# Cross-attention and mixture-of-experts layer: layer-norm statistics, bias split and weight pieces placed elsewhere, fewer index copies

## What is computed

```python
def reference(x, ctx, abundance, w_in, b_in, w_out, b_out, gate_w, expert_bias, w1, w2, w3):
    # x [2, 1024, 256], ctx [2, 64, 256], 16 heads of 16, 8 experts, hidden 704, top 2
    q = layernorm(x) @ w_q.T + b_q;  k = ctx @ w_k.T + b_k;  v = ctx @ w_v.T + b_v
    scores = einsum('bhqd,bhkd->bhqk', q, k) / 4 + log(abundance)[:, None, None, :]
    x = x + (softmax(scores) @ v) @ out_proj_weight.T + out_proj_bias
    xf = layernorm(x).reshape(2048, 256)
    s = softmax(xf @ gate_w.T);  sel = top_k(s + expert_bias, 2)
    # tokens sorted by expert; routed = xf[token] * s[token, expert]
    # out[token] += (silu(routed @ w1[e]) * (routed @ w3[e])) @ w2[e]
    return x + out
```

## Time and profile before

| what | us |
|---|---|
| median of 3 runs (lowest, highest) | 438.52 (437.52, 440.04) |
| the profiled execution | 439.58 |
| its span, from the first instruction to the last | 437.8 |
| PE, DVE, ACT, POOL busy | 354.1, 240.5, 197.6, 237.0 |

### The profile page before, as it was taken

How to read it: one execution, slowest core, us unless ns; L and a number is a source line. 1 busy time by engine, 2 the same in 40 slices (tenths; PEclk the granted TensorE clock), 3 DMA queues, 4 the chain that set the end, 5 groups by cost and what they waited for, 6 DMA issues and landing times.

```text
span 437.8 us, 9846 instructions
## 1 busy us (share of the span) xinstructions
PE 354.1 (81%) x2573; PEld 266.7 (61%) x2574; DVE 240.5 (55%) x615; ACT 197.6 (45%) x343; POOL 237.0 (54%) x295
## 2 busy tenths in 40 slices
PE   2676699999888862128899999999999999999830
PEld 1455578888876752115567776767677767776620
DVE  1655776576665247925555555555555555555400
ACT  3567477787877632004333334333344444333300
POOL 6319786675775755041345565655555555664340
PEclk9886898898999655558999999999999999999995
DMA  7923676767895721023777777777777777889546
GB/s 235 317 26 96 187 213 162 198 184 162 241 214 167 238 60 20 0 73 64 122 125 135 136 138 136 135 134 135 133 134 134 135 138 130 133 136 143 95 57 204
DMA packets 121523, 61.53 MB, mean 141 GB/s; under 512 B 97170, under 2 KB 116124, under 8 KB 121468
## 3 DMA queue, kind: packets, MB, share of 16 engines
q1 hardware_dynamic: 113408, 50.45, 49.0%
q0 software_dynamic: 7488, 10.39, 15.6%
q10 hardware_dynamic: 604, 0.41, 0.4%
HBM read 28.88 MB, written 11.60 MB: 92 GB/s over the span
## 4 chain that ended last, share of the span: by engine, by line
PE 68%; DVE 10%; DMA 6%; ACT 6%; issue 4%; POOL 1%; SPq 0%; POOLq 0%; ACTq 0%; DVEq 0%
PE sc L1389 11%; PE sc L1390 10%; PE sc L1391 10%; PE bank L1286 6%; PE bank L1405 5%; PE bank L1408 5%; PE bank L1407 4%; PE bank L1328 3%; PE ptps L1342 3%; ACT w_lo L770 2%; DMA acc<-xn,put_now 2%; DMA arena<-x 2%; PE bank L1299 2%; PE ptps L1270 1%; DMA arena<-arena 1%
## 5 line engine op out<-in xcount | busy, mean ns | idle before, releaser
L1389 PE MATMUL sc<-w_hi,arena 128*128 x312 | 99.1, 318 | 11.8 <-DMA arena<-x 9.9
L605 POOL DMA_INDIRECT acc<-xn,put_now x39 | 62.5, 1601 | 74.4 <-DVE xn L1139 63.4
L1390 PE MATMUL sc<-w_hi,arena 128*128 x312 | 98.8, 317 | 0.0
L1391 PE MATMUL sc<-w_lo,arena 128*128 x312 | 98.7, 316 | 0.0
L797 ACT ACTIVATE arena<-sc,slot_score 128x352 f32<-128x352 f32 x78 | 43.2, 553 | 117.2 <-PE sc L1391 116.1
L1126 DVE SCALAR_TENSOR_TENSOR arena<-sc,slot_score,arena 128x352 f32<-128x352 f32 x78 | 45.5, 584 | 86.0 <-ACT arena L797 84.8
L515 POOL TENSOR_TENSOR w_lo<-stage_w,w_hi 128x1408 f16<-128x1408 f32 (+1 forms) x32 | 72.5, 2275 | 23.9 <-ACT w_hi L632 20.8
L1405 PE MATMUL bank<-w_hi,arena 128*128 x234 | 63.8, 273 | 3.8 <-DMA arena<-arena 2.0
L1408 PE MATMUL bank<-w_lo,arena 128*128 x234 | 61.7, 273 | 0.0
L574 POOL DMA_INDIRECT arena<-table,get_now x39 | 41.3, 1060 | 31.2 <-POOL get_now L571 31.2
L1407 PE MATMUL bank<-w_hi,arena 128*128 x195 | 53.2, 273 | 0.0
(11 more groups left out here) (187 smaller groups left out, 580.5 us busy)
## 6 DMA issues: line engine op xcount, KB each, us to landing
stage_w<-in_L_ffn_w SPq DMA_DIRECT2D x16, 704.0 KB, 4.7
stage_w<-in_L_ffn_w SPq DMA_DIRECT2D x8, 384.0 KB, 4.6
stage_w<-in_L_ffn_w SPq DMA_DIRECT2D x8, 256.0 KB, 2.6
acc<-arena SPq DMA_DIRECT2D x16, 128.0 KB, 1.8
table<-xn SPq DMA_DIRECT2D x16, 128.0 KB, 2.1
arena<-in_x SPq DMA_DIRECT2D x2, 768.0 KB, 8.2
stage_w<-in_L_ffn_w SPq DMA_DIRECT2D x16, 64.0 KB, 2.5
arena<-arena SPq DMA_TRANSPOSE x53, 5.2
```

The costliest lines, as they stand in the source:

```text
L605: pool.indirect_dma_start(out=acc[:, :], out_offset=bass.IndirectOffsetOnAxis(ap=put_now[par][:, 0:1], axis=0), in_=y_sb[par], in_offset=N ...
L1389: pe.matmul(ps[:, c, :], gT[par][:, k, :], w_hi[:, cols], start=k == 0, stop=False)
L1390: pe.matmul(ps[:, c, :], gT[par][:, KD + k, :], w_hi[:, cols], start=False, stop=False)
L1391: ins = pe.matmul(ps[:, c, :], gT[par][:, k, :], w_lo[:, cols], start=False, stop=k == KD - 1)
```

## The change

1. `first_stats`/`first_moments` of group 0 go behind the column and context copies, group 1 ahead of `tokens_low(0)`, group 2 ahead of `queries_low(1)`; group 3 and the bias split go from step 1 into step 0. On ACT `queries_evict(0)` goes ahead of `rows_apply(2)`. POOL's `first_scales` of group 3 goes from step 2 to step 1.
2. `plan` and `late` are new: two pieces in steps 2 and 3 and in 13 to 15, the last four in steps 16 and 17. ACT casts piece 0 inside `first_step`, ahead of `tokens_high(3)`. POOL takes piece 28 in step 16 and pieces 29 to 31 in step 17.
3. PE's wait ahead of L1270 asks for one count of `pt_sb` less: for the first half of the tile's probabilities, which lie in the columns that L1270 writes, and no longer for the second.
4. EARLY is 14. In steps 18 and 19 ACT does `rows2_apply` ahead of other work.
5. Six gathers outside the loop read their column of the index list in place.

```diff
-        EARLY = T - 4
+        EARLY = T - 2
...
-        plan = [[], []] + [[0], [0, 1], [0], [1, 0], [1, 1]] * 3 + [[]] * 3
-        late = [[]] * T + [[0], [0], [1], [1]]
+        plan = [[], [], [0, 1], [0, 1], [0], [1, 0], [1, 1]] + [[0], [0, 1], [0], [1, 0], [1, 1]] + [[0]] + [[0, 1]] * 3 + [[]] * 4
+        late = [[]] * T + [[0, 0], [1, 1], [], []]
...
             def step(t):
-                if t == 2:
+                if t == 1:
                     first_scales(*LN_GROUPS[3], 4)
...
+                for n in at_step[t]:
+                    piece_low(n)
+                if t == T:
+                    pool.wait_ge(s["o_ps"], T - 1)
+                    piece_low(LATE)
                 if t == T + 1:
                     pool.wait_ge(s["o_ps"], T)
-                for n in at_step[t]:
-                    piece_low(n)
-                if t > T:
-                    for n in late_step[t - 1]:
+                    for n in range(LATE + 1, len(PIECES)):
                         piece_low(n)
...
-                pool.tensor_copy(get_now[par][:, :], idx_get[:, col]).then_inc(s["get_idx"], 1)
-                pool.wait_ge(s["get_idx"], j + 1)
-                carry(pool)
+                if dyn:
+                    pool.tensor_copy(get_now[par][:, :], idx_get[:, col]).then_inc(s["get_idx"], 1)
+                    pool.wait_ge(s["get_idx"], j - 5)
+                    carry(pool)
+                    rows = get_now[par][:, 0:1]
+                else:
+                    rows = idx_get[:, col]
...
                 queries_high(2)
+                piece_high(at_step[0][0])
                 tokens_high(3)
...
-                for n in at_step[t][0:1]:
+                if t > T and here(t, 3):
+                    rows2_apply(t - 3)
+                if late_step[t]:
+                    act.wait_ge(s["pt_ps"], 2 * (t - 1))
+                for n in (at_step[t] + late_step[t])[t == 0:1]:
                     piece_high(n)
+                if t == T + 1:
+                    for n in late_step[t][1:]:
+                        piece_high(n)
...
+                if t == T:
+                    piece_high(late_step[t][1])
...
                 if t == 0:
                     queries_low(2)
                     tokens_low(3)
+                    link(dve.tensor_copy(bo16[:, :], bo_all))
+                    link(dve.scalar_tensor_tensor(out=bo_rest, in0=bo16[:, :], scalar=low_rows[:, 0:1], in1=bo_all,
+                                                  op0=ALU.mult, op1=ALU.add))
+                    dve.tensor_copy(bo16[:, :], bo_rest).then_inc(s["bo_s"], 1)
+                    for n in range(8, 12):
+                        first_stats(n)
                     queries_low(3)
-                    for n in range(*LN_GROUPS[2]):
+                    for n in range(12, T):
                         first_stats(n)
-                    first_moments(*LN_GROUPS[2])
+                    first_moments(*LN_GROUPS[3])
...
                     pe.wait_ge(s["xn2_ready"], bt + 1)
-                    pe.wait_ge(s["pt_sb"], 2 * min(t - 1, T))
+                    pe.wait_ge(s["pt_sb"], 2 * min(t - 1, T) - 1)
```

More of the change, by code:

```diff
@@ L682, in _ @@
             tokens_high(1)
+            queries_evict(0)
             rows_apply(2)
-            queries_evict(0)
             queries_high(1)
@@ L748, in step @@
                     tokens_high(5)
[L749 to L757, removed]
+                if t <= T and here(t, 3):
+                    rows2_apply(t - 3)
                 for n in at_step[t][1:]:
@@ L761, in step, with rows2_apply @@
                     probs_across(t - 1, 1)
[L762 to L765, removed]
+                if t == T:
+                    piece_high(late_step[t][1])
+            def rows2_apply(bt):
+                act.wait_ge(s["ln2_shift"], bt + 1)
+                if bt >= 2:
+                    act.wait_ge(xn2_st[bt % 2], loads_of(bt - 2))
+                    act.wait_ge(s["x2t_ps"], bt - 1)
+                act.activation(xn2[bt % 2][:, :], xs[:, bt, :], ACT.Identity, bias=nmr2[:, 0:1], scale=rs2[:, 0:1])\
+                    .then_inc(s["xn2_ready"], 1)
             def probs_across(bt, c):
@@ L833, in _ @@
             dve.tensor_copy(ident16[:, :], ident[:, :]).then_inc(s["ident16_s"], 1)
-            for tt in range(*LN_GROUPS[0]):
-                first_stats(tt)
-            first_moments(*LN_GROUPS[0])
             dve.wait_ge(s["cols_ps"], 1)
@@ L847, in _ @@
             dve.wait_ge(s["consts"], N_CONST_MASK)
+            for tt in range(*LN_GROUPS[0]):
+                first_stats(tt)
+            first_moments(*LN_GROUPS[0])
             dve.tensor_reduce(pair_half, head_mask.rearrange("p (i r) -> p r i", r=2), AX.X, ALU.add)\
@@ L869, in spread_keys @@
                                       None, ALU.mult).then_inc(s["kb_dve"], 1)
+            for tt in range(*LN_GROUPS[1]):
+                first_stats(tt)
+            first_moments(*LN_GROUPS[1])
             tokens_low(0)
@@ L895, in _ @@
             queries_low(0)
-            for tt in range(*LN_GROUPS[1]):
-                first_stats(tt)
-            first_moments(*LN_GROUPS[1])
             dve.wait_ge(s["kt_ps"], 1)
@@ L903, in _ @@
             dve.tensor_copy(gateT[:, :, :], pt_ps2[:, 512:512 + KD * E].rearrange("p (k e) -> p k e", k=KD)).then_inc(s["gT_sb"], 1)
+            for tt in range(*LN_GROUPS[2]):
+                first_stats(tt)
+            first_moments(*LN_GROUPS[2])
             queries_low(1)
@@ L910, in _ @@
                                 .broadcast_to([P, B, 2, S2])).then_inc(s["ctx_sb"], 1)
+            dve.wait_ge(s["bo_load"], 16)
+            dve.wait_ge(s["consts"], N_CONST_PREP)
             n_r = [0]
@@ L996, in step @@
                     tokens_low(5)
-                    for n in range(*LN_GROUPS[3]):
-                        first_stats(n)
-                if t == 1:
-                    first_moments(*LN_GROUPS[3])
-                if t == 1:
-                    dve.wait_ge(s["bo_load"], 16)
-                    dve.wait_ge(s["consts"], N_CONST_PREP)
-                    link(dve.tensor_copy(bo16[:, :], bo_all))
-                    link(dve.scalar_tensor_tensor(out=bo_rest, in0=bo16[:, :], scalar=low_rows[:, 0:1], in1=bo_all,
-                                                  op0=ALU.mult, op1=ALU.add))
-                    dve.tensor_copy(bo16[:, :], bo_rest).then_inc(s["bo_s"], 1)
                 if t == T + 3:
```

5 lines of the change are left out of this document (1 added, 4 removed).

## The result

| what | before | after |
|---|---|---|
| median, us | 438.79 | 422.11 |
| lowest, highest of 4 runs | 437.52, 440.04 | 419.65, 425.54 |
| profiled execution (its span) | 439.58 (437.8) | 419.65 (417.9) |
| ratio, 95% interval | | 0.9625 [0.9551, 0.9700] |

The forecast of 423.0 and its range held. The profiled execution of after is the lowest of its four, so its trace shows 19.9 us of gain in the span where the medians show 16.7. Lines have moved: L1258 is now L1267, L1270 L1279, L1286 L1295, L1313 L1322, L1328 L1337, L770 L780, L1005 and L1008 are L1004 and L1007, L925 is L940, L933 L948, L951 L966, L965 L980, L1031 L1040, L1091 L1100.

The account below looks back on a forecast made before the run. PE (68% of the chain) was held up by DVE's statistics and its wait ahead of L1270. A to F sum to 14.4 us, taking 438.52 to 424.1; 1.1 off for the clock gives 423.0, range 417 to 430.

Parts of the forecast that it names:

- A: Start to L1313 of step 2: DVE's statistics and bias split moved earlier gain 5.9 us, bounds 4.4 and 6.9.
- B: L1313 of step 2 to the next scores: low clock behind PE's standing goes, 1.3 us, between 0 and 1.3.
- C: PE's wait ahead of L1270 shrinks, steps 4 to 17: 6.1 us, less 0.6 for steps 13 to 15, so 5.5.
- clock in the steps: Two low-clock stretches within the steps cost 5.1 us before; a quarter counted as gone, 1.1 us (estimate).
- D: L1286's end, tile 15 (X), to its LN2 statistics: L925 waits for POOL's last piece; -1.5 us, between 0 and -2.2.
- E: LN2 statistics of tile 15 to `sel`: POOL idle beside DVE, last group smaller; gain 2.8 us, between 1.5 and 3.6.
- F: First gather: index copy dropped, most of the gap being the indirect DMA's own; gain 0.4 us, between 0.1 and 0.9.
- 0.9 to 1.15 behind the scores: Sign of being right: L1286 stands 0.9 to 1.15 us behind the scores in steps 4 to 15.
- rival 2: Wait ahead of L1270 moves instead of going, C gives nothing: 429.6 us, about 428.5 with quiet clock; chance 0.15.
- rival 1: Clock stays at 2.4 GHz through all steps, since PE hardly stands: 419.0 us; chance 0.20.
- slower than before by more low stretches: Start leaves the clock at 1.2 GHz through the steps; five more long low stretches give 441 us; chance 0.04.
- moved work trades places: Moved work only trades places: A and C fall to a third, B to nothing; 433.0 us, worst no change; chance 0.09.

Follow-up runs that it names:

- e9: Kernel after with all eight group 3 statistics and the moments first, then the bias split, then queries_low(3), in step 0; 417.88 us, ratio to before 0.9504.
- e1: Kernel before with one edit: the wait ahead of L1270 asks for one count of pt_sb less; 430.25 us, ratio to before 0.9859.
- a_again: Kernel after run once more, unchanged, in a later group; 421.00 us, ratio to before 0.9598.
- e6: Kernel after with the copies into get_now back ahead of all gathers; 417.44 us, one execution.
- e7: Kernel after with EARLY = 12; 426.26 us, one execution.
- e4: Kernel after with step 17's residual and LN2 statistics of tile 15 ahead of gate_shift of the early group; 423.08 us, ratio to before 0.9654.
- e2: Kernel after with the old wait ahead of L1270 put back; 427.26 us, ratio to before 0.9779.
- e3: Kernel after with the bias split behind the statistics of group 3 and their moments in step 0; 420.15 us, ratio to before 0.9636.
- e5: Kernel after with POOL's last two pieces (30 and 31) behind the LN2 of tile 15; 420.75 us, ratio to before 0.9592.

## Why the prediction was right, point by point

| term | predicted | measured in the profiled runs |
|---|---|---|
| A, start to L1313 of step 2 | 5.9 | 6.05 |
| B, from there to the scores of step 3 | 1.3 | 1.27 |
| C, wait ahead of L1270, steps 4 to 15 | 4.8 | 4.4 (steps 4 to 14) |
| C, steps 16 and 17 | 0.7 | 3.05, clock included |
| clock in the steps | 1.1 | 3.0 (steps 3 to 15) |
| D, X to `mv` of tile 15 | -1.5 | -1.28 |
| E, to `sel` | 2.8 | 2.76 |
| F, first gather | 0.4 | 0.43 |
| expert loop | 0 | 0.2 |

**A and B** held in size and mechanism: the cast ended with piece 0, as the step said. The size of A is in part luck: the queries of tile 4 came at 33.9 for 34.9, and L1322 at 40.97 for 41.1, since low clock in the scores of step 2 (1.06) and in L1295 (2.49) took back the 0.9 in between. Two things in A were thinner than they looked. Its start was late: the load of x for tiles 2 and 3 ended at 10.7 and DVE's statistics of that group had to wait for it, without a loss that the rows show further on. And its upper bound was wrong. It put 1.0 on a cast that slips in ahead of the piece, though by its own times DVE came there at 26.9 (26.5 and 0.4), 1.6 ahead of the piece's end; it came at 25.5, 2.3 ahead, and e9, without that wait, shows 9.0 (47.02 to 38.02), some of it clock.

**C** held in mechanism and, where it can be measured, in size: 0.47 for the 0.5 of steps 4 to 11, 0.24 for the 0.35 of steps 12 to 14. The scores of step 15 come ahead of its own wait, so the 4.4 leave that step out; there L1295 stands 0.85 behind the scores, before 1.22. The sign "0.9 to 1.15 behind the scores" failed in two steps: in 6 and 11, where ACT has a large piece ahead of L780, it is 1.44. But L1286 stood 2.01 behind there before, so these steps gained as much as the others, and ACT's piece took nothing from the edit there. Nor are ACT's two pieces in steps 13 to 15, for which the prediction took off 0.6, the reason for 0.24 instead of 0.35: e1 has the same 0.24 with the old tables. And the prediction misread a row in its argument against rival 2. In step 3 ACT's large piece does not stand ahead of the L770 that L1286 waits for. Timeline of before:

```profile
50.92 0.60 ACT L770 ACTIVATE w_lo<-ptps 128x512 f32<-128x512 f32 x1 [1.30 <-PE ptps L1342]
...
52.82 1.37 ACT L632 ACTIVATE w_hi<-stage_w 128x1408 f16<-128x1408 f32 x1
```

What C gave in steps 16 and 17 can't be told from the clock: from the scores of step 15 to X, after gains 3.05 and a_again, the same program, 1.35.

**The clock** is the term that was under-sized, 1.1 for 3.0 and about 1.5 more at L1295 of tile 15. The profiled run lies at 419.65; rival 1, counted from the same profile of before, gives 439.58 - 14.4 - 5.1 = 420.1, so in size it is what this trace shows. In kind it is not: the clock still fell twice in the steps. Nor is it fixed by the program. Four runs of after spread from 419.65 to 425.54 with mean granted clocks from 0.914 to 0.897, and e6, after and e7 show that the same instructions between the scores of steps 3 and 15 meet none, one or two low stretches. By the medians 15.5 was forecast and 16.7 measured; by the profiled pair it is 15.5 for 19.9. That the forecast of 423.0 came within 0.9 of the median owes something to luck, since nothing in it said how much low clock the other executions would meet.

**D and E** held, each by its own step: L940, 1.39 long, ended 0.13 behind POOL's last piece, L966 of the early group took 0.22 instead of 1.68, and L940 and L948 of the last group 0.17 each instead of 1.25 and 0.86. e4 shows that D's loss was not needed.

**The rivals.** That the wait ahead of L1270 only moves is ruled out by e1 and e2, slower than before by more low stretches did not happen: the slowest execution of the kernel after, 432.67, lies below the fastest of before on that chip, 435.32. That moved work trades places was true of the cast and of part D, as forecast, and of e3 and e5, not of the change as a whole.

**Open** is what makes a low stretch fall within the steps. On the page "TensorE: Matmul & The Clock Gate" (section "What's actually happening") the Trainium skill says that the throttled state is the default and activity releases it. The traces agree in part at the start, where low stretches follow PE's waits (after: 2.49 us of standing up to 31.8, low from 32.1), though in e9 PE stood 2.50 up to 30.8 and the clock stayed full until 36.0. In the steps of after and e7 PE was busy for 3.30 of the 3.30 us of one low stretch each, and e6 had none with the same instructions, so the rows do not show what sets it. Not tested by itself is what ACT's `rows2_apply` ahead of other work gives; by the code it stands so in steps 17 and 18, not 18 and 19.

## What to carry to other kernels

When an instruction on VectorE that copies, casts or reads two SBUF tiles is moved, list GpSimd's instructions at the new place as well as at the old one, the next one too: here the gap between two pieces gave 1.9 to 2.4 us at PE for casts of 0.3, and the place that ran into the second piece gave nothing. A semaphore wait can ask for the half that it needs; the gain is the same from both sides (4.4 us here), and it is cheap to show so by adding the edit to the old kernel and taking it from the new one. Compare steps that ran at full clock with the same steps at full clock, since whole times of kernels that differ by 0.4 us here lay 2% apart (417.44 and 426.26) with where the clock fell; and do not take off half of a low stretch where the engine would have waited at full clock.

## What the runs showed of the hardware that was not expected

- A DVE instruction and a chain of two POOL pieces take turns by whole instructions: L961 of 1.09 us took 2.56 and the two pieces 4.08 instead of 3.19, though they began within 0.02 us of each other.
- The granted clock differs between executions of the same instructions: in programs that are the same up to step 16 there was none (e6), one of 3.4 us (after) or two of 3.3 and 3.4 us (e7) between the scores of steps 3 and 15, and ahead of those, from 14 us on, 3.4 and 6.8 us in after and in e6, and 13.7 in e7.
- An indirect DMA of POOL starts 0.93 us behind the end of the instruction that made its index (L1100) even without a copy, and 0.30 behind the end of an earlier one.
- The conflict holds for a POOL instruction on a single column too: L545 (128x1) took 1.17 us beside DVE's two-input L958 (after), 1.05 beside L943 (before), and 0.26 in most tiles.
